# States and shears with time outermost, one gathered copy of a unit's states, and one key buffer

## What is computed

```python
def step(carry, inp):
    z, s = carry
    u_t, dt_t, k_t, Bz_t, Bx_t, Cz_t, Cx_t = inp
    dtE = dt_t[:, :, None, None]
    S = 1.0 / (1.0 + dt_t[..., None] * k_t[..., None] + (dt_t * dt_t)[..., None] * A)
    z = S[..., None] * (z - dtE * A[None, :, :, None] * s + dtE * (Bz_t[..., None] * u_t[:, :, None, :]))
    s = s + dtE * z + dtE * (Bx_t[..., None] * u_t[:, :, None, :])
    y = jnp.einsum('bhn,bhnd->bhd', Cz_t, z) + jnp.einsum('bhn,bhnd->bhd', Cx_t, s)
    return ((z, s), y)
```

## Time and profile before

| | |
|---|---|
| median of 3 runs (lowest to highest) | 2361.71 us (2357.69 to 2366.44) |
| the profiled execution, its own time | 2356.95 us |
| its span, first to last instruction | 2355.2 us |
| busy in the span: PE, PEld | 2026.4 us (86%), 1059.6 us (45%) |
| busy in the span: DVE, ACT, POOL | 2053.6 us (87%), 1080.7 us (46%), 83.4 us (4%) |

### The profile page before, as it was taken

The page is one execution under the profiler, slowest core; times in us unless marked ns, Lnnn a source line. Parts: engine busy times, 40 slices in busy tenths (PEclk is TensorE's granted clock), DMA queues, the critical chain, the costliest instruction groups (busy, mean ns, idle before and its releaser), DMA issues. The chain is left out here.

```text
span 2355.2 us, 78715 instructions
## 1 busy us (share of the span) xinstructions
PE 2026.4 (86%) x31266; PEld 1059.6 (45%) x31266; DVE 2053.6 (87%) x5467; ACT 1080.7 (46%) x1700; POOL 83.4 (4%) x28
## 2 busy tenths in 40 slices
PE   6777469999999999899999999998999998357886
PEld 2333124444444444444444544444444444246675
DVE  6887589998999999999989999998999996487774
ACT  4665225544454444445444544444554544024453
POOL 0000000000000000000000000000000000153300
PEclk9898779999999999999999999999999999578997
DMA  4455644565555465545655554655456443443300
GB/s 137 176 212 177 177 93 105 130 143 130 128 129 129 121 142 128 123 106 133 143 128 130 126 128 112 146 132 123 105 131 145 108 97 85 149 160 134 143 27 27
DMA packets 224664, 300.27 MB, mean 127 GB/s; under 512 B 96784, under 2 KB 114192, under 8 KB 218128
## 3 DMA queue, kind: packets, MB, share of 16 engines
q1 hardware_dynamic: 174416, 212.11, 35.8%
q10 hardware_dynamic: 48704, 78.68, 12.9%
q0 software_dynamic: 1152, 4.19, 0.5%
HBM read 240.85 MB, written 50.86 MB: 124 GB/s over the span
## 5 line engine op out<-in xcount | busy, mean ns | idle before, releaser
L670 PE MATMUL m_ps_a<-m_valT,m_w_bc 128*128 128x512 f32 x2048 | 967.1, 611 | 50.4 <-DMA m_valT<-scratch_valT 33.8
L670 PEld LDWEIGHTS m_ps_a<-m_valT,m_w_bc 128*128 128x128 f32 x2048 | 366.8, 191 | 510.0 <-issue 503.6
L822 ACT ACTIVATE m_sq<-m_ps_a 128x512 f32<-128x512 f32 x256 | 152.9, 597 | 540.5 <-PE m_ps_a L670 536.8
L962 DVE TENSOR_TENSOR m_prod<-m_psi,m_shear 128x128 f32<-128x128 f32 x960 | 368.4, 384 | 0.0
L966 DVE TENSOR_TENSOR m_psi<-m_psi,m_prod 128x128 f32<-128x128 f32 x960 | 367.9, 383 | 0.0
L681 PE MATMUL m_ps_s<-m_sq,m_head_sum 128*32 128x512 f32 x512 | 267.9, 606 | 24.4 <-ACT m_sq L822 24.4
L693 PE MATMUL m_ps_g<-m_q,m_k 32*64 32x64 f32 x8192 | 124.8, 234 | 45.0 <-issue 37.2
L693 PEld LDWEIGHTS m_ps_g<-m_q,m_k 32*64 32x64 f32 x8192 | 108.9, 135 | 101.0 <-ACT m_dX L844 55.4
L823 ACT ACTIVATE m_raw<-m_ps_a 128x512 f32<-128x512 f32 x256 | 151.9, 593 | 0.0
L221 PE MATMUL ps_w<-p_xnT,w_in 128*128 128x512 f32 x256 | 119.4, 620 | 16.5 <-ACT gate L284 16.3
L756 PEld LDWEIGHTS m_ps_y<-m_q,m_X 32*16 32x16 f32 x7168 | 103.8, 93 | 53.3 <-issue 53.3
(11 more groups left out here) (143 smaller groups left out, 3085.4 us busy)
## 6 DMA issues: line engine op xcount, KB each, us to landing
m_scale<-scratch_norm SPq DMA_DIRECT2D x256, 256.0 KB, 5.3
m_w_bc<-in_w_bcT ACTq DMA_DIRECT2D x252, 256.0 KB, 3.8
m_shear<-scratch_n_alpha SPq DMA_DIRECT2D x64, 256.0 KB, 5.2
m_shear<-scratch_beta SPq DMA_DIRECT2D x256, 64.0 KB, 3.7
m_det<-scratch_gd SPq DMA_DIRECT2D x256, 64.0 KB, 4.5
scratch_gateT<-gate SPq DMA_DIRECT2D x8, 1024.0 KB, 3.9
scratch_valT<-val SPq DMA_DIRECT2D x8, 1024.0 KB, 4.5
scratch_svgT<-svg SPq DMA_DIRECT2D x8, 1024.0 KB, 5.8
```

Source lines behind the costliest of these rows:

```text
L670: mm = pe.matmul(ps_a[j % 2].ap(), w_bc[:, j, kt, :], valT[:, kt, :], start=(kt == 0), stop=(kt == KI - 1), skip_group_check=True)
L822: act.activation(sq[:, j % 2, :], ps_a[j % 2].ap(), ACT.Square).then_inc(sq_ready.sem, sq_ready.step)
L962: dve.tensor_tensor(prod.ap(), psi_t[half][:, :, :, :, t], shear_t[half][:, :, :, t].unsqueeze(1).to_broadcast([P, 2, 2, HALF * NC]), ALU. ...
```

## The change

`psi` and `shear` get time as their outermost dimension and the column (group of the half, chunk) as their innermost, so that the operands of a step are runs of 32, 64 or 128 elements. Keys and queries need one group's states with time innermost: ScalarE copies them into a new tile `psi_g` (`gather_psi`, one ACTIVATE of 2080 elements in a partition, read with a stride of 128 floats), one buffer for all units. `project` stores `n_alpha` and `beta` side by side in a new scratch tensor `shear` as well; SP loads both for one group into one buffer `stage` (for the first four groups of row 0 into the two `raw` buffers), and ScalarE lays them into `shear` with two ACTIVATEs that write with a stride (`lay_shear`). `k` has one buffer, and `kt` and `kT` become views of `scale`, so that the load of the next `scale` waits for the queries and for dX instead of for the scaling. On VectorE the product with `det` stands ahead of the keys, and `log_sum` ahead of the masks.

```diff
-        psi = sb("psi", [P, 2, 2, HG, NC, C + 1])
-        shear = sb("shear", [P, 2, HG, T])
+        psi = sb("psi", [P, 2, C + 1, 2, 2, HALF * NC])
+        psi_g = sb("psi_g", [P, 2, 2, NC, C + 1])
+        shear = sb("shear", [P, 2, C, 2, HALF * NC])
+        stage = sb("stage", [P, 2, T])
-        k = [sb(f"k{s}", [P, 2, T]) for s in range(2)]
+        k = sb("k", [P, 2, T])
-        kt = sb("kt", [P, 2, T])
+        kt = scale[:, 0:2, :]
+        kT = scale[:, 2:4, :]
-        kT = sb("kT", [P, 2, T])
...
-                    sp.wait_ge(scaled.sem, scaled.at(b, group - 1))
+                    sp.wait_ge(q_ready.sem, q_ready.at(b, group - 1))
+                    sp.sem_inc(sp_passed, 1)
+                    sp.wait_ge(dX_made.sem, dX_made.at(b, group - 1))
...
-                load_n_alpha(0, 1)
+                load_e_end(0)
                 for group in range(HALF, HG):
-                    load_beta(0, group)
-                load_e_end(0)
+                    sp.wait_ge(shear_ready.sem, shear_ready.at(0, group - 1))
+                    load_shear(0, group, stage)
                 load_u(0, 0)
                 compact_norms(0, 0)
...
                         if not last:
-                            if group % HALF == 0:
-                                sp.wait_ge(stepped.sem, stepped.at(b, group // HALF))
-                                load_n_alpha(b + 1, group // HALF)
-                            load_beta(b + 1, group)
+                            sp.wait_ge(shear_ready.sem, shear_ready.at(b, HG - 1 if group == 0 else HG + group - 1))
+                            load_shear(b + 1, group, stage)
...
+                def lay_shear(b, group, src, loads=None):
+                    cols = slice(group % HALF * NC, (group % HALF + 1) * NC)
+                    dst = [shear[:, group // HALF, :, comp, cols].rearrange("p t c -> p c t") for comp in range(2)]
+                    act.wait_ge(shear_in.sem, shear_in.at(b, (loads or group + 1) * HP - 1))
+                    act.wait_ge(stepped.sem, stepped.at(b - 1, group // HALF))
+                    act.activation(dst[0], chunks(src[:, 0, :]), ACT.Copy, scale=A[:, group:group + 1])
+                    act.activation(dst[1], chunks(src[:, 1, :]), ACT.Copy).then_inc(shear_ready.sem, shear_ready.step)
+
+                def gather_psi(b, group):
+                    half, cols = group // HALF % 2, slice(group % HALF * NC, (group % HALF + 1) * NC)
+                    act.wait_ge(stepped.sem, stepped.at(b, group // HALF))
+                    act.wait_ge(raw_used.sem, raw_used.at(b, group - 1))
+                    act.wait_ge(coef_ready.sem, coef_ready.at(b, group - 1))
+                    act.activation(psi_g.ap().rearrange("p r k c t -> p (r k) c t"),
+                                   psi[:, half, :, :, :, cols].rearrange("p t r k c -> p (r k) c t"),
+                                   ACT.Copy).then_inc(psi_ready.sem, psi_ready.step)
...
                 for group in range(HALF):
-                    scale_beta(0, group)
+                    lay_shear(0, group, first_stage[group], HALF)
...
                 norms(0, 0)
                 for group in range(HALF, HG):
-                    scale_beta(0, group)
+                    lay_shear(0, group, stage)
                 det_log(0, 0)
                 det_inverse(0, 0)
+                gather_psi(0, 0)
                 for j in range(NJ):
                     evacuate(0, 1, j)
...
                             norms(b, group + 2)
+                        if not last and group == 0:
+                            lay_shear(b + 1, 0, stage)
                         if here:
                             copy_kT(b, unit)
...
-                        if not last and group == 0:
-                            scale_beta(b + 1, 0)
                         if not last and group < LAST:
-                            scale_beta(b + 1, group + 1)
+                            lay_shear(b + 1, group + 1, stage)
...
                             det_inverse(b, group + 2)
+                            gather_psi(b, group + 2)
...
-                            dve.tensor_tensor(prod.ap(), psi_t[half][:, :, :, :, t],
-                                              shear_t[half][:, :, :, t].unsqueeze(1).to_broadcast([P, 2, 2, HALF * NC]),
-                                              ALU.mult).then_inc(steps.sem, steps.one())
+                            dve.tensor_tensor(prod.ap().rearrange("p r k c -> p r (k c)"),
+                                              psi[:, half, t].rearrange("p r k c -> p r (k c)"),
+                                              shear[:, half, t].rearrange("p k c -> p (k c)").unsqueeze(1
+                                              ).to_broadcast([P, 2, 2 * HALF * NC]), ALU.mult).then_inc(steps.sem, steps.one())
...
                         dve.wait_ge(own.sem, b_scaled)
-                        dve.wait_ge(kT_made.sem, kT_made.at(b, 2 * (group - 2) + 1))
-                        dve.wait_ge(g_made.sem, g_made.at(b, group - 2))
+                        dve.wait_ge(psi_ready.sem, psi_ready.at(b, group))
+                        dve.wait_ge(kT_made.sem, kT_made.at(b, 2 * (group - 1) + 1))
+                        dve.wait_ge(g_made.sem, g_made.at(b, group - 1))
```

More of the change, by code:

```diff
@@ L526, in by_chunk @@
         def by_chunk(v):
-            return v.ap().rearrange("p r (c t) -> p r c t", c=NC)
+            return v.rearrange("p r (c t) -> p r c t", c=NC)
         def over_rows_of(v):
             return chunks(v).unsqueeze(1).to_broadcast([P, 2, NC, C])
+        first_stage = [raw[s][:, 2 * n:2 * n + 2, :] for s in range(2) for n in range(2)]
         def spread(src, parts=N):
@@ L935, in _ @@
                     for comp in range(2):
-                        dve.memset(psi[:, row, comp, :, :, 0:1], 1.0 if row == comp else 0.0).then_inc(own.sem, own.one())
+                        dve.memset(psi[:, :, 0, row, comp, :], 1.0 if row == comp else 0.0).then_inc(own.sem, own.one())
                 dve.wait_ge(own.sem, own.n)
@@ L1115, in body @@
                             dve.wait_ge(X_ready.sem, X_ready.at(b, group * (NC - 1) + c))
+                        if not (last and group == LAST):
+                            log_sum(b, group + 1)
                         for two in range(2):
@@ L1123, in body @@
                             advance(1)
-                        if not (last and group == LAST):
-                            log_sum(b, group + 1)
                         advance(end_at - done)
```

94 lines of the change are left out of this document (41 added, 53 removed).

## The result

The changed kernel is slower: 2470.34 us median (2465.2 to 2472.33, 4 runs) against 2361.93 us for the kernel before on the same chip, a ratio of 1.0478 (95% interval 1.0451 to 1.0505). The forecast was 2429 us, with a range up to 2462: the direction and most of the places were right, the size was not. The profiled execution has a span of 2468.7 us, 113.5 us more than before.

A forecast was written before the change was run, and what follows sets the result against it. TensorE and its pauses were taken to bound the kernel: 2357 profiled + 59 gather stall + 13 start - 5 faster steps = 2424, forecast 2429 us as a median (chance 0.62), range 2345 to 2462.

The forecast's parts named there:

- stall of the gather: ScalarE's gather ahead of the fourth evacuation stalls TensorE g - 2.3 us a unit; with g 3.5 us, +59 us after pauses.
- Edits at nothing: One key buffer, keys housed in scale, shear layouts by two ACTIVATEs, and SP's shear loads and waits: no cost counted.
- TensorE and its pauses set the pace: In the scan stage TensorE and its pauses under "issue" bound the units; VectorE's time is mostly hidden.
- rival of pauses as disguised waits: 62.2 us of TensorE's pauses are really VectorE's lateness and go, with the stall hidden: 2308 us median, chance 0.18.
- What pauses swallow: TensorE's existing pauses cover part of the 74.4 us gather stall: 7.9 us at line 744, 7.2 at line 670.
- The start: Ahead of the first unit, norms queued behind staged shear loads and layouts delay VectorE: +8 to +20 us, taken +13.
- The faster steps: VectorE's scan steps read runs, 384 to 293 ns; only TensorE's 5.3 us wait for keys is gained: -5 us.
- a third or half of the 62 us of pauses goes: Partial case of the rival that pauses are waits for VectorE: 2325 to 2340 us.
- the steps stay at 384 ns: Rival: contiguous steps gain nothing, the start loses its 11.6 us gain, the gather's stall stays: 2441 us median, chance 0.06.
- part 3: The start of the scan stage: staged loads, layouts and norms against faster first steps, 5.8 us less; +13 us net.

The follow-up runs named there:

- e4: Kernel before with contiguous steps alone, no gather or layouts, and without the loop's steps except the last of each half: 2319.13 us, ratio 0.9879.
- e11: Changed kernel with two buffers for the staged shears, every layout left in place: 2462.26 us, ratio 1.0422.
- e12: Changed kernel with two stage buffers and a row's first layout moved from ahead of the key copy to behind the logarithm: 2453.54 us, ratio 1.0386.
- e6b: Changed kernel with the first unit's norms sent after one of four staged shear loads, run beside the control: 2461.80 us against 2473.60.
- e5: Kernel before with one more store of beta for each row in project, into an unused scratch tensor: 2356.82 us, ratio 1.0024.
- e7: Changed kernel with beta stored only once for each row in project: 2469.20 us, 4.4 below the control.
- e3: Kernel before with the contiguous steps alone, no gather or layouts, keys made with a constant tile: 2321.83 us, ratio 0.9892.
- e1: Changed kernel with the gather reading 2080 neighbouring elements instead of ones 512 bytes apart: 2392.31 us, ratio 1.0176.
- e9: Changed kernel with the gather done twice, once into an unused tile: 2750.54 us, a single run.
- mended kernel: Changed kernel with early gather, two stage buffers, layouts moved off the key copy, norms sent earlier, beta stored once, first-unit evacuations reordered: 2338.02 us, ratio 0.9942.

## Why the prediction was wrong in size

The mechanism held: the gather ended late and TensorE waited for it. Sizes failed at three steps. The stall of the gather was put at 59 us and was 81. The layout and SP's wait at place 1 were put at nothing, under "Edits at nothing", and were 15 us on top of the rest (24 by themselves). A second store of beta in `project`, about 5 us, was no term at all.

**TensorE and its pauses set the pace: right.** The rival of pauses as disguised waits is refuted for 60 of its 62 us (e4). The Trainium skill's "Runtime: NRT & Kernel Launch", section "Instruction fetch mechanics", says that the cost of fetching the next block of instructions is mostly hidden; by that the pauses would have another cause. The runs rule out VectorE as that cause, since the pauses stay when its busy time falls from 1574 to 1138 us, and tie them to places in the program; none shows whether they are fetches.

**The stall of the gather: right formula, low price.** The stall is g - 2.3 us a unit; I took g = 3.5 between 2.0 and 3.8, adding VectorE's stride penalty to ScalarE's pace. It is 3.82: (3823 - 181)/2080 = 1.75 ns an element, which is VectorE's strided slope of 1.74 and not the sum of the two. With it the formula gives 1.52 us; places 2 to 7 lost 1.47. That is 20 us over 62 units. The Trainium skill's "Vector Engine (DVE) Microarchitecture Reference", section "Measured stream behaviour on trn2", has 1.73 ns for a source that hops each element; the gather agrees, though the page is about another engine.

**What pauses swallow: half right.** Place 0, with the pauses at line 670, lost nothing, as assumed (7.2 us). The 7.9 us at line 744 did not swallow anything: the pauses were there again, 10.7 us at line 741.

**Edits at nothing: wrong, 15 us.** For the layout ahead of the key copy I named six matmuls of line 670 as cover and 2 us a row as its price without. The cover held for what it was named for: in the unit shown above the chunk states (line 700) follow those matmuls at 1289.61 without a wait. What I left out is that dX stands on ScalarE behind the same layout, and behind y and its four stores; it came 1 us later. For SP's wait I wrote that it is for a layout of the unit before and that the norms queued behind it come later. At place 1 this is wrong: on ScalarE that layout stands right behind the square roots, so the norms are ready first, 0.6 us after their square roots begin, and wait on SP for the layout and the load. Place 1 lost 3.58 - 1.47 = 2.1 us more than the other places, in seven rows: 0.7 to 1.2 by SP (e11), 0.8 by the layout (e12).

**The start: right.** +13 forecast, +14.8 measured. The mechanism named, norms behind staged loads and layouts, is shown for 6.5 to 7.4 of it by e6b and for 10.5 by e11; the rest is argued.

**A store that was not costed.** The diff shows that `project` stores beta twice. It was no term of the sum, and is about 5 us (e5, e7) of the 9.5 by which `mix` began later.

**The faster steps: -5 in the stage was right for the wait that it was taken from, and too much for this kernel.** Alone the steps give back that wait at place 7, 6 us in e3; the other 19 at the row's ends came with shorter pauses at the start of a pass, of which no run shows the cause. In the changed kernel the keys waited for ScalarE instead of VectorE, and place 7 lost 1.12 us instead of 1.47: little of the 5 is left. That place 0 gained 5 us there is another thing, and the equal number is chance.

**Two sums of the rivals** do not come out as written. If a third or half of the 62 us of pauses goes, the median is 2349 or 2339 us, not 2325 to 2340. If the steps stay at 384 ns, the start loses the 5.8 us that part 3 counted and not 11.6, but the 5 us at the keys go as well, so that sum is about 1 us below the one given.

By the runs the sum is 55 units x 1.47 (places 1 to 7 of seven rows, six units of the last) = 81, 15 more at place 1, -0.7 x 7 = -5 at place 0, which makes the 90 of the stage within rounding, and 14.8 + 9.5 ahead of it: 115, where the span grew by 113.5. The top of the stated range had the dear gather, but not place 1 and the store together.

## What to carry to other kernels

An engine that is busy half the time is not free at every moment: ask in which gap of its order the added instruction lands, and whether a step that the pace-setting engine waits for stands right behind it. Here the same 3.8 us cost 88 us of the stage more in one gap than in another, one evacuation earlier. Follow the added instruction down the order of its engine to every result that another engine waits for, not only to the next one. A wait put into a queue that also carries other work is charged with all that stands behind it, so give the buffer it waits for a second copy, and go through every line of a diff, stores outside the loop included.

## What the runs showed of the hardware that was not expected

- ScalarE takes 3823 ns for 2080 elements that lie 512 bytes apart, and 1920 ns for neighbours (e1): 1.75 against 0.84 ns an element. Writes with a stride cost as well: 512 elements in 1102 to 1185 ns (lines 814 and 813) against 630 for a contiguous ACTIVATE of that size in the earlier trace rows.
- A wait that recurs in each unit was charged twice where it was long: with 1.1 us on average (the changed kernel) the stage was granted 1.00 of full speed, with 4.6 us (e9, a single run) 0.91, which added 1.9 us of slower matmuls to each unit.
- TensorE's pauses under "issue" inside scores, chunk states and outputs (62.2 us before, 59.8 in e4) stand ahead of the same matmuls from row to row, in the kernel before, in the changed one and in e4, multiples of about 125 matmul records apart.
- The pauses of about 3 us at line 670 all stand where TensorE has gone back to the start of the loop (six before and in the changed kernel, one in e3, none in e4, four in the mended kernel). In the kernel before one of them, from 1421.2 to 1424.3, falls on a stretch in which the DMA engines are fully busy (a share of 1.04 between 1420 and 1425 us). A full load is not needed for them: in the changed kernel five of the six fall on shares of 0.58 to 0.84. Why they come and go was not tried.
